# Statistics of half the rows made in one block, block loads a step ahead, reloads in parts, ScalarE's ramps ahead of its high parts

## The reference, cut to what matters

```python
xn  = layernorm(x)                                   # over the last axis
s   = attention over the batch axis, for each of 1024 positions, with q = xn, plus xn
Wg, Wu, Wd = NF4[codes] * scales                     # 2752 x 1024, 2752 x 1024, 1024 x 2752
ffn = (silu(xn @ Wg.T) * (xn @ Wu.T)) @ Wd.T
out = x + s * silu(ffn)
```

## Time and profile before

| | us |
|---|---|
| median of 3 runs (2650.83 to 2657.51) | 2653.19 |
| the profiled execution, its own time | 2647.06 |
| its span | 2645.3 |
| TensorE busy | 2440.1 (92%) |
| VectorE busy | 1671.4 (63%) |
| ScalarE busy | 1011.9 (38%) |
| GpSimd busy | 166.1 (6%) |

### The profile page before, as it was taken

The page is one execution under the profiler, slowest core; times in us unless marked ns, Lnnn a source line. Parts: engine busy times, 40 slices in busy tenths (PEclk is TensorE's granted clock), DMA queues, the critical chain, the costliest instruction groups (busy, mean ns, idle before and its releaser), DMA issues.

```text
span 2645.3 us, 30451 instructions
## 1 busy us (share of the span) xinstructions
PE 2440.1 (92%) x11214; PEld 1113.7 (42%) x11214; DVE 1671.4 (63%) x2929; ACT 1011.9 (38%) x1303; POOL 166.1 (6%) x110
## 2 busy tenths in 40 slices
PE   2459999998899898999999999999999999999999
PEld 1224444443344343444444444444444444444444
DVE  6767887977688765787888788656451331341341
ACT  5467766657576643445445442111001001001000
POOL 3540000000000000000000000000011011011011
PEclk9689999998899899999999999999999999999999
DMA  6254565756566538666565654325877767766864
GB/s 221 100 172 157 187 195 179 221 179 203 182 204 196 195 128 331 214 225 203 185 215 190 202 192 171 129 85 201 335 285 281 322 263 275 324 267 270 326 267 159
DMA packets 176017, 571.15 MB, mean 216 GB/s; under 512 B 23968, under 2 KB 49232, under 8 KB 158076
## 3 DMA queue, kind: packets, MB, share of 16 engines
q1 hardware_dynamic: 140876, 280.82, 31.2%
q10 hardware_dynamic: 34992, 288.37, 29.0%
HBM read 380.38 MB, written 188.75 MB: 215 GB/s over the span
## 4 chain that ended last, share of the span: by engine, by line
PE 68%; DVE 12%; DMA 7%; issue 6%; ACT 3%; POOL 2%; SPq 2%; DVEq 0%; POOLq 0%; ACTq 0%
PE ps L1560 38%; PE ps L1689 29%; DMA arena<-xnsc 3%; DVE arena L1226 3%; DMA isc<-arena 2%; DVE arena L1160 1%; ACT arena L727 1%; POOL arena L680 1%; DVE arena L1135 1%; SPq L505 1%; DMA arena<-in_gu 1%; DVE arena L1219 1%; DVE arena L1394 1%; DVE st L1075 1%; DMA xsc<-arena 1%
## 5 line engine op out<-in xcount | busy, mean ns | idle before, releaser
L1560 PE MATMUL ps<-arena 128*128 128x512 f16 x7200 | 1595.5, 384 | 107.6 <-ACT arena L902 52.1
L1560 PEld LDWEIGHTS ps<-arena 128*128 128x128 f16 x7200 | 710.2, 99 | 980.7 <-ACT arena L902 58.4
L1689 PE MATMUL ps<-arena 128*128 128x512 f16 x3696 | 797.9, 379 | 0.0
L727 ACT ACTIVATE arena<-arena,bias_t 128x1024 f32<-128x1024 f32 (+1 forms) x520 | 574.3, 1141 | 53.2 <-DMA arena<-in_gu 33.7
L1689 PEld LDWEIGHTS ps<-arena 128*128 128x128 f16 x3696 | 361.6, 98 | 436.3 <-issue 0.4
L1226 DVE TENSOR_TENSOR arena<-arena 128x512 f16<-128x512 f32 x364 | 248.9, 686 | 72.7 <-ACT arena L861 71.2
L692 POOL TENSOR_TENSOR arena<-arena 128x512 f32<-128x512 f32 x64 | 81.8, 1286 | 2376.4 <-DMA arena<-in_xt 2072.7
L1043 ACT ACTIVATE arena<-arena,e_d 128x512 f32<-128x512 f32 x48 | 34.6, 721 | 424.3 <-DVE arena L1489 219.4
L902 ACT ACTIVATE arena<-ps,gate_back 128x512 f32<-128x512 f32 x84 | 57.3, 682 | 348.2 <-PE ps L1560 348.2
L1219 DVE CAST arena<-arena 128x512 f16<-128x512 f32 x308 | 126.5, 421 | 40.8 <-DMA isc<-arena 38.3
L912 ACT ACTIVATE arena<-arena,gate_back 128x512 f32<-128x512 f32 x84 | 60.4, 720 | 208.6 <-DVE arena L1391 179.7
...
## 6 DMA issues: line engine op xcount, KB each, us to landing
isc<-arena SPq DMA_DIRECT2D x308, 256.0 KB, 2.4
...
arena<-in_gu ACTq DMA_DIRECT2D x43, 512.0 KB, 4.2
wdsc<-arena SPq DMA_DIRECT2D x77, 256.0 KB, 2.3
arena<-in_x SPq DMA_DIRECT2D x32, 512.0 KB, 6.9
```

Source lines behind the costliest of these rows:

```text
L727: a_.activation(buf, src, ACT.Prelu, bias=bias_t[:, i:i + 1], scale=scale, alpha=alpha).then_inc(ramps, 1)
L1560: ins = t_.matmul(ps[:, bank, :], wreg[:, b, w, wa, k, :], xreg[:, j, o, k, xa, :], start=start and (k, wa, xa) == (0, 0, 0), stop=stop an ...
L1689: ins = t_.matmul(ps[:, bank, :], ring_w[b][:, k, wa, g, :], ring_i[b][:, k, xa, :], start=first and (k, wa, xa) == (0, 0, 0), stop=r not ...
```

## The change

- `STAT_AT`, `ROOTS_AT`: the statistics of all 16 tiles are made in steps 4 (six tiles), 6 (five) and 7 (five), one tile a slot, by a load of their own through the same two slots. All 16 aggregates and one chain of roots for all of them follow in step 8, slot 1. `NORM_AT` moves to steps 8, 10 ... 22; the tiles are loaded a second time, and VectorE does one instruction a tile there, in slots 4 and 5.
- The x jobs move to steps 26, 27, 30, 31, 34, 35, 38, 39. Those with j = 0 have their high parts cast on VectorE, and all their items in slots 0 to 2 (`SOON_CUT`). Those with j = 1 keep ScalarE's high parts (`X_ACT`), of which the first three now stand ahead of p1's copy.
- SP asks for a block a step ahead: at the start of the step before the pair, and, for the second of a pair, after the stores of the first.
- `reloads(s, part)`: the reloads of steps 41 to 45 in up to four parts spread over ScalarE's step.
- ScalarE does the first ramps of a step, then an evacuation, then the weights' high parts; `W_CUT` moves VectorE's low parts of weights one slot later.
- Small ones: the first down-stage items of step 44 in slot 5, a scale load in step 43 instead of 40, two memsets behind a product, `p6_bank` from step 24.

```diff
-NORM_AT = {6 + 2 * i: (16 + 2 * i, 17 + 2 * i) for i in range(8)}
-XJOB_AT = {s: (2 + i // 4, i % 4) for i, s in enumerate([s for s in SPARE if s >= 22][:8])}
+STAT_AT = {4: range(16, 22), 6: range(22, 27), 7: range(27, 32)}
+ROOTS_AT = 8
+NORM_AT = {8 + 2 * i: (16 + 2 * i, 17 + 2 * i) for i in range(8)}
+XJOB_AT = {s: (2 + i // 4, i % 4) for i, s in enumerate([s for s in SPARE if s >= 24][-8:])}
+X_ACT = [XJOB_AT[s] for s in XJOB_AT if PASS[s][1]]
...
+SOON_CUT = [0, 8, 13, 18, 18, 18, 18]
-W_CUT[9], W_CUT[5], W_CUT[6] = [0, 0, 2, 3, 4, 5, 9], [0, 0, 1, 2, 3, 4, 5], [0, 0, 1, 2, 3, 4, 6]
+W_CUT[9], W_CUT[5], W_CUT[6] = [0, 0, 2, 3, 4, 5, 9], [0, 0, 0, 1, 3, 4, 5], [0, 0, 0, 1, 3, 4, 6]
+W_CUT[8] = [0, 0, 0, 2, 3, 4, 8]
...
+            def load_stat(tt):
+                if tt < 18:
+                    sp.wait_ge(e_lo, 5 * 7)
+                else:
+                    sp.wait_ge(stat, 2 * (tt - 18) + 2)
+                sp.dma_start(nat[nat_slot(tt)], x[...]).then_inc(nat_in[nat_slot(tt)], 16)
...
-                if s in XJOB_AT:
-                    load_blocks(("x",) + XJOB_AT[s])
+                if s + 1 in XJOB_AT and s not in XJOB_AT:
+                    load_blocks(("x",) + XJOB_AT[s + 1])
...
                 for c in jobs_at(s):
                     for o in X_ORDER:
                         store_stage(c, o)
+                if s + 1 in XJOB_AT and s in XJOB_AT:
+                    load_blocks(("x",) + XJOB_AT[s + 1])
...
+                if s == 3:
+                    load_stat(16)
+                    load_stat(17)
+                for tt in STAT_AT.get(s, ()):
+                    if tt + 2 < 32:
+                        load_stat(tt + 2)
...
-                    if s == 41:
-                        act.wait_ge(prod, prod_at(40, "p5"))
-                        load_xb(0, 5)
-                        load_xb(0, 6)
-                        act.wait_ge(prod, prod_at(39, "p3"))
-                        load_w(0, 4, 7)
-                        load_w(0, 2, 4)
-                    elif s == 42:
-                        act.wait_ge(prod, prod_at(41, "r"))
-                        act.wait_ge(prod, prod_at(40, "p3"))
-                        for o in (0, 4, 2, 3):
-                            load_xb(0, o)
+                if (s, part) == (41, 0):
+                    act.wait_ge(prod, prod_at(40, "p5"))
+                    load_xb(0, 5)
+                elif (s, part) == (41, 1):
+                    load_xb(0, 6)
+                elif (s, part) == (41, 2):
+                    act.wait_ge(prod, prod_at(39, "p3"))
+                    load_w(0, 4, 7)
+                elif (s, part) == (41, 3):
+                    load_w(0, 2, 4)
+                elif (s, part) == (42, 0):
+                    act.wait_ge(prod, prod_at(41, "r"))
+                    act.wait_ge(prod, prod_at(40, "p3"))
+                    load_xb(0, 0)
+                elif (s, part) == (42, 1):
+                    load_xb(0, 4)
...
+                if on_act:
+                    for o in (0, 1, 2):
+                        x_high(("x",) + XJOB_AT[s], o)
                 if s < TOTAL:
                     p1_copy(s)
+                ramps_of(s, 0, 2)
+                if half_tile_at(s, "p6"):
+                    evac(*half_tile_at(s, "p6"))
                 if 4 <= s < 40 and u + 1 != LAST:
                     for o in ([0, 4, 5], [1, 3, 6, 2])[j]:
                         w_high(u + 1, o)
+                if s < TOTAL:
+                    reloads(s, 1)
...
-                if s in NORM_AT and slot == 3:
-                    lnorm(NORM_AT[s], 2)
+                for tt in list(STAT_AT.get(s, ()))[slot:slot + 1]:
+                    stats(tt)
+                if s == ROOTS_AT and slot == 1:
+                    all_roots()
+                if s in NORM_AT and slot >= 4:
+                    normal(NORM_AT[s][slot - 4])
```

128 lines of the change are left out of this document (82 added, 46 removed).

## The result

The changed kernel takes 2607.37 us (median of 4 runs, 2605.57 to 2609.82), the kernel before, run beside it, 2653.97 (2650.83 to 2657.51): the ratio is 0.9825, with a 95% interval of 0.9808 to 0.9842. The profiled execution took 2605.87 us; its span is 41.3 us shorter than that of before.

The account below looks back on a forecast made before the run. TensorE was taken as the bound, losing time in three places; gains of 49 + 5 + 10 = 64 us from 2647 give 2583, plus 3 for the median: 2586 us, own range 2565 to 2605, wider range 2553 to 2622.

Parts of the forecast that it names:

- the rival of 2615: Whole kernel: VectorE becomes the bound; blocks gain 29, statistics -5, reloads 10, 34 us in all; chance 0.19.
- Blocks a step ahead, casts on VectorE: Steps 22 to 41: earlier block requests and half the high parts on VectorE win 49 of 66.0 us lost.
- LayerNorm: Steps 4 to 21: moving the statistics ahead costs some 13 us new and removes 18.0; 5 us gained.
- the 18.0 us go: Steps 7 to 21: all gaps and clock loss vanish, those on the codes' load too; 18.0 us.
- Reloads in parts: Steps 42 to 45: asking for reloads in parts leaves stores slowed, not stopped; 10 of 16.5 us won.
- reloads in parts bring nothing: Rival, steps 42 to 45: bytes bind or queues take turns anyway; 2596 us, stores over 8 us in step 42; chance 0.12.
- Ramps ahead of high parts: ScalarE's order in a step: later high parts of weights cost nothing while VectorE's 8 us of spare lasts; 0 us.
- the slower rival: Every step with j = 0: VectorE waits 5.1 us for the weights' high parts; about 2665 us; chance 0.05.
- clock: Sign, x stretch (steps 22 to 41): granted clock rises to 0.97 or more, from 0.94.
- VectorE over 0.95: Sign, steps 24 to 39: VectorE is busy over 0.95 of the time.
- stores under 8 us: Sign, steps 41 to 44: stores take under 8 us.
- c21 gaps in steps 5 and 9: Sign: TensorE's gaps on c21 stand in steps 5 and 9; 2.6 and 5.8 us, each with 1.7 of clock.

Follow-up runs that it names:

- n_req12: Changed kernel with a pair's second block asked for behind the first job's fifth store, later pairs' first block right behind the previous x job: 2592.60 us.
- u_requests: Changed kernel with each x block asked for at the start of its own step again: 2611.09 us.
- u_casts: Changed kernel with all eight x jobs' high parts on ScalarE again, which also moves VectorE's items to three a slot: 2624.46 us.
- u_stats: Changed kernel with the old LayerNorm, each pair of tiles in one piece in slot 3, no statistics in steps 4, 6, 7: 2628.52 us.
- a_ramps: Kernel before with only ScalarE's first ramps ahead of its high parts and VectorE's low parts of weights a slot later: 2654.23 us against 2653.21.
- c_dve: Changed kernel with all eight x jobs' high parts cast on VectorE, all items in slots 0 to 2: 2609.9 us.

## Why the prediction was right or wrong

**The time.** 2586 was forecast and 2607.37 measured, inside the range of 2553 to 2622 but 2 us above the forecast's own range of 2565 to 2605; of a gain of 64 us 41 came on the spans. By the number alone the rival of 2615 lies nearer. The signs of the two large terms were right, their sizes partly, and the reasons less so than the sum.

*Blocks a step ahead, casts on VectorE: 49 forecast, 34.2 measured.* The silu gaps came out as worked out: none above 2.75 us, the clock at 0.97, the block 12.4 us into step 27 where 9 was said and 21.8 stood. Missing in the sum was what the first block's request collides with: it was costed from the side of the block alone, while seven stores of an i job stand behind it on SyncE's queue. The first of them take 6.6 to 10.2 us, and VectorE waits 15.3 us for its stages. Of the 17.1 us of c21 gaps, which no term had, 6.4 follow these waits; the other 10.7 stand behind the steps with 18 items in slots 0 to 2, and mostly stay when the stages' waits go (`n_req12`). Of the 377.6 us of this stretch, for 19 steps at 18.14 and 1.7 of transposes, 31 are still lost, where 17 were said. `u_requests` shows how little the early request is worth net, 3.7 us; `u_casts` shows that the casts, with the items' place that goes with them, carry 17.1, by the chain that the term described (first job done, second request, landing, silu). The jobs' later steps, and the three high parts ahead of p1's copy, were not tested by themselves.

*LayerNorm: 5 forecast, 7.5 measured in steps 4 to 22.* -9.5 in steps 4 to 9 and +17.0 in 9 to 22 against 13 and 18. The sum is near in part by luck. A gap came in step 5, but on the silu and not on c21 (5.35 where before had 2.30; `u_stats`, without the statistics there, has 3.07), and the one on c21 in step 7 and not in step 9 (6.97 for 5.8). And "the 18.0 us go" put into the LayerNorm's term also what the new order on ScalarE gives; taken back from the changed kernel, the LayerNorm costs 21.2, not 5. `a_ramps`, which has the new order with the old LayerNorm, loses 15.2 us in steps 4 to 22: the two do not go together.

*Reloads in parts: 10 forecast, nothing measured.* This is the term that failed outright, by its reason as by its size. The longest store of steps 41 and 42 in the chain takes 11.44 us with the parts and 11.48 with the reloads together; the stretch moves 323 GB/s now, 324 before. The prediction read the 13.80 us of the earlier trace rows as a store held by big loads of another queue; four loads of scales stood ahead of it on its own queue, and with the reloads together but the scales asked for later the store of that place takes 6.25. The rival "reloads in parts bring nothing" held for this stretch. One of its two reasons was taken from the Trainium skill (DMA: Bandwidth & Descriptors, Queues, rings and completion order), by whose rule of turns between queues parts on ScalarE's queue change nothing for a store on SyncE's. That consequence agrees with the runs; the size does not: by turns a store would take about twice its median of 2.4, which is an estimate, and 11.44 and 8.36 are measured.

*Ramps ahead of high parts: 0 forecast; 22.9 when taken back, nothing alone.* The term looked at what VectorE might newly wait for (14.0 us in 8 waits now, all hidden, so the slower rival did not come: the codes' wait is 3.9 us at the longest, where that rival had 5.10 in every step). It did not look at what ScalarE no longer waits for, 54 us of standing for VectorE's scaling, which the trace of before shows. The slower rival's own sum does not close either: 18 x 1.7 of clock is 31 us, and 12 were added, so that its time would have been 2685.

*VectorE becomes the bound (2615)* was near in time but not in its reason: VectorE is busy 0.87 of steps 26 to 40, not over 0.95, and 8 us more work on it cost 1 (`c_dve`).

*The signs.* Right: the first block's wait gone, clock, no c21 gap in steps 13, 17, 21, silu gaps under 5. Wrong: VectorE over 0.95, stores under 8 us, c21 gaps in steps 5 and 9.

**The parts don't add.** Taken back one at a time they cost 22.9 (ramps), 21.2 (statistics), 17.1 (casts), 3.7 (requests) and -2.0 (reloads), 63 in all, where the whole change brought 46.6. For the ramps both sides are measured, 22.9 with the other parts and nothing alone; that the statistics and the casts hang on the others in the same way is argued, not shown. Open stay: whether the scales' later load alone closed the gap of 10.69 us in step 42, and what makes the c21 gaps of steps 31 and 39.
